# Two score products of a unit, issued together or with transposes or value products between them

## The chip, the cores and the metric

One core of one Trainium2 chip runs the whole program. The metric is the device time of one execution in microseconds (us), as a median over several executions.

## The reference

The reference applies two transformer layers, one after the other, to x of shape (8, 512, 256), with 16 heads of 16 elements. Only the attention of the first layer matters here; the second has the same outline with a key mask in place of the distance term.

```python
qkv = (h @ Wqkv).reshape(B, L, 3, H, hd)             # h: layer norm of x, scaled and shifted
scores = jnp.einsum('bhqd,bhkd->bhqk', q, k) / np.sqrt(hd)
scores = scores - torus_dist[:, None, :, :] * torus_scale[None, :, None, None]
attn = jax.nn.softmax(scores, axis=-1)
out = jnp.einsum('bhqk,bhkd->bhqd', attn, v)
x = x + out @ Wout
x = x + (jax.nn.gelu(layer_norm(x) @ W1 + b1) @ W2 + b2)
```

## The kernel before, in words

The kernel writes every engine's instruction stream by hand and ties the streams with semaphores. It goes through 16 passes: passes 0 to 7 are the first layer, one batch row each, and passes 8 to 15 the second layer. The second layer has a short form, taken when the mask lets all keys but the last 128 drop out of consideration, and with these inputs it is the one that runs. The change touches the code that the first 8 passes use. (The long form of the second layer shares this code, but doesn't run here.)

A pass of the first layer has 37 steps, k = 0 to 36. Its attention is cut into 32 units; a unit is one head and one half of the queries (256 of them). A unit goes through these stages.

- **Scores** (TensorE, `scores`, L869): two products of 97 rows, each 128 queries by 512 keys. They alternate between two PSUM banks, so the product t may start when VectorE has read the product t - 2 (`scores_used`). Unit k is computed in step k. Units 0 and 1 of the next pass are computed ahead, in steps 33 and 35. After the first pass, units 18 and 21 are computed in the middle of the dense work of steps 17 and 20.
- **Shift** (VectorE, `shift_scores`, L1401): for each product, it combines the product with the bias and keeps the row extremum, 128x512 elements, about 0.69 us. The bias is made on GpSimd (`make_bias`, L624), for every fourth unit on ScalarE (L1101), and lies in one of two buffers.
- **Subtract** (GpSimd, `subtract_max`, L631): two operations a unit, into `shifted`.
- **Turn** (TensorE, `turn_unit`, L881): eight 128x128 transposes, four to a PSUM bank. The four of a bank are called a pair here. Unit u is turned in step u + 2. It waits for GpSimd (`shifted_ready`), and each pair z waits until ScalarE has read the pair z - 2 (`probs_ready`).
- **Exponential** (ScalarE, `exps`, L1112): one operation for each pair.
- **Value products** (TensorE, `attend`, L896): for four units at once, 32 instructions, in steps 7, 11, 15, 19, 23, 27, 31 and 35. Two steps later come two transposes (L905), and VectorE divides (L1422, L1426).

TensorE works strictly in the order of its list. In each step that order is: the two scores, then the value products if it is their step, then the eight transposes, then the two transposes of the output, then dense pieces from the table `FIRST` (up projection L777, output projection, query and key projection) and pieces of the down projection from `FIRST_DOWN` (L797). VectorE's step is: divide, the two shifts, the dense pieces of the step before, then a part of a layer norm (`FIRST_NORM`, steps 4, 6, 11 and 13). ScalarE's step k is: the output copy, the dense pieces of step k, the exponentials of unit k - 1, and a bias for unit k + 2 where that is its turn. The table of step 15 holds `t2`, two groups of transposes for the second norm, each of which costs ScalarE two operations ahead of the exponentials. Steps 17 and 20 hold four up projections each, and ScalarE loads another table of functions there and loads the first back afterwards.

SyncE loads the query and key rows of a group of eight units when the scores of an earlier group are ready (`load_group`).

Of the kernel before, what the change touches and what calls it, by code (L numbers as in the profile page):

```python
# [18 lines left out]
def build(nc, d, out):  # L19
    B, L, D = d["x"].shape  # L20
# [15 lines left out]
    UNITS = 2 * H  # L36
    HALF = L // 2
    GQ = 2 * G
# [24 lines left out]
    AHEAD = {33: 0, 35: 1}  # L63
# [25 lines left out]
    ATTEND = 7  # L89
# [3 lines left out]
    TURN = 2  # L93
# [3 lines left out]
    def begun(n, u):  # L97

        return 0 < n < B and u in AHEAD.values()

    def amid(n, k):
        return n > 0 and k in AMID
# [24 lines left out]
    def pieces(table, k, n):  # L127
        return [(p, pass_of(p, n)) for p in table.get(k, []) if pass_of(p, n) is not None]

    with ExitStack() as ctx:  # L130
# [6 lines left out]
        def sem(name):  # L137
            return ctx.enter_context(nc.semaphore(name))
# [124 lines left out]
        s = {name: sem(name) for name in names}  # L263

        def short(n):
            return n >= B and not chosen["any"]
# [506 lines left out]
        def _(pe):  # L773
# [14 lines left out]
            def down_chunks(m, first, last):  # L788
                for i, c in (divmod(x, FCH) for x in range(first, last)):
                    piece = ("down", i)  # L790
                    if i == 0 and c == 0:
                        for last_up in range(DENSE):
                            piece_read(pe, ("up", FCH - 1 - last_up), m)
                        pe.wait_ge(s["down_loaded"], 48 if m < B else 96)
                    if c == 0:
                        bank_free(pe, piece, m)
                    mm = pe.matmul(bank_of(piece, m)[:, 0:D], hidden[:, c, P * i:P * i + P],  # L797
                                   w_down[:, c, :], start=(c == 0), stop=(c == FCH - 1))
                    if c == FCH - 1:
                        mm.then_inc(s["dense_ready"], 1)  # L800
# [56 lines left out]
            def rows_loaded(n, g):  # L857
                pe.wait_ge(s[f"group{g % 2}_loaded"], ROWS_LOADED * (2 * n + g // 2 + 1))

            def scores(n, u):  # L860
                g, half, j = u // 8, u // 4 % 2, u % 4
                if u % 8 == 0:
                    rows_loaded(n, g)
                for i in range(2):
                    t = 2 * u + i
                    if n > 0 or t > 1:
                        pe.wait_ge(s["scores_used"], TILES * n + t - 1)
                    q0 = HALF * half + P * i
                    pe.matmul(score_bank[t % 2], q_rows[0:KROWS, g % 2, j // 2, q0:q0 + P],  # L869
                              k_rows[0:KROWS, g % 2, j // 2, j % 2, :], start=True, stop=True).then_inc(s["scores_ready"], 1)  # L870

            def turn_unit(n, u):
                pe.wait_ge(s["shifted_ready"], UNITS * n + u + 1)
                for pair in range(2):
                    z = 2 * u + pair
                    if n > 0 or z > 1:
                        pe.wait_ge(s["probs_ready"], TILES * n + z - 1)
                    for kk in range(2):
                        kt = 2 * pair + kk
                        for i in range(2):  # L880
                            mm = pe.transpose(turned_bank[z % 2][:, HALF * kk + P * i:HALF * kk + P * i + P],  # L881
                                              shifted[:, u % 3, i, P * kt:P * kt + P], ident[:, :])
                    mm.then_inc(s["turned_ready"], 1)
# [25 lines left out]
            def pair_scores_of(n, q):  # L909

                g, pair = q // 2, q % 2
                if pair == 0:
                    few_loaded(pe, n, g)
                if q > 0 or n > B:
                    pe.wait_ge(s["peaks_ready"], H // 2 * (n - B) + q)
                else:
                    pe.wait_ge(s["scores_used"], TILES * B)
                for t in range(TT):
                    mm = pe.matmul(score[:, t // 2, HALF * (t % 2):HALF * (t % 2) + HALF],  # L919
                                   q_rows[0:KROWS, g, pair, P * t:P * t + P],  # L920
                                   k_rows[0:KROWS, g % 2, pair, :, key_slot(g)], start=True, stop=True)
                mm.then_inc(s["scores_ready"], 2 * TT)

            def turn_peaks(n, q):
                pe.wait_ge(s["split_ready"], H // 2 * (n - B) + q + 1)
                pe.transpose(score_bank[0][0:4 * TT, 0:P], split_peak[:, :].bitcast(F32), ident[:, :])\
                    .then_inc(s["peak_turned"], 1)
# [13 lines left out]
            def attend_heads(n, g):  # L941
                if g == 0:
                    piece_read(pe, ("v", TT - 1), n)
                    pe.wait_ge(s["vmask_ready"], n - B + 1)
                pe.wait_ge(s["probs_ready"], TILES * n + TT * HG * (g + 1))
                pe.wait_ge(s["attn_ready"], GQ * n + 2 * g)
                for j in range(HG):
                    mm = pe.matmul(pv_bank[SLOT * j:SLOT * j + SLOT, :], v_ext[:, TT - 1, HG * g + j, :],  # L948
                                   head_probs[:, (HG * g + j) % RING, :], start=True, stop=True,
                                   skip_group_check=True)  # L950
                mm.then_inc(s["probs_used"], 2)
# [37 lines left out]
            def turn(n):  # L989
                if short(n):  # L990
                    for p in range(HEAD_STEPS):
                        attended = p >= 6 and p % 2 == 0
                        if 2 <= p < 2 + H // 2:
                            pair_scores_of(n, p - 2)
                        for k in range(3 * p, 3 * p + 2):
                            for piece, m in pieces(HEADS, k, n):
                                dense(piece, m)
                            if k in HEADS_DOWN:
                                down_chunks(n - 1, *HEADS_DOWN[k])
                        if attended:  # L1000
                            attend_heads(n, (p - 6) // 2)
                        if 4 <= p < 4 + H // 2:
                            turned_scores_of(n, p - 4)
                        if 2 < p < 2 + H // 2:
                            turn_peaks(n, p - 2)
                        for piece, m in pieces(HEADS, 3 * p + 2, n):
                            dense(piece, m)
                        if p == 2:

                            turn_peaks(n, 0)  # L1010
                        if 3 * p + 2 in HEADS_DOWN:
                            down_chunks(n - 1, *HEADS_DOWN[3 * p + 2])
                        if attended:
                            heads_to_tokens(n, (p - 6) // 2)
                    return
                table, down = (FIRST, FIRST_DOWN) if n < B else (ANY, ANY_DOWN)
                for k in range(STEPS):
                    if k < UNITS and not begun(n, k) and not (n < B and amid(n, k - 1)):
                        scores(n, k)
                    if n + 1 < B and k in AHEAD:  # L1020
                        scores(n + 1, AHEAD[k])
                    if k >= ATTEND and (k - ATTEND) % 4 == 0 and (k - ATTEND) // 4 < GQ:
                        attend(n, (k - ATTEND) // 4)
                    if TURN <= k < TURN + UNITS:
                        turn_unit(n, k - TURN)
                    if k >= TOKENS and (k - TOKENS) % 4 == 0:
                        to_tokens(n, (k - TOKENS) // 4)
                    for i, (piece, m) in enumerate(pieces(table, k, n)):
                        if n < B and amid(n, k) and i == 2:
                            scores(n, k + 1)  # L1030
                        dense(piece, m)
                    if n > 0 and k in down:
                        down_chunks(n - 1, *down[k])
                for gq in range(GQ):
                    if TOKENS + 4 * gq >= STEPS:
                        to_tokens(n, gq)

            def epilogue():
                for piece, m in listed(ANY if chosen["any"] else HEADS, N):
                    dense(piece, m)  # L1040
                down_chunks(N - 1, 0, TT * FCH)

            run(pe, prologue, turn, epilogue)

        @block.scalar
# [576 lines left out]
```

## Time and profile before

| | us |
|---|---|
| median of 3 runs | 1400.09 (1396.74 to 1400.62) |
| the profiled execution's own time | 1405.66 |
| its span, first to last instruction | 1403.9 |
| busy: TensorE matmul | 1294.1 (92%) |
| busy: TensorE weight load | 994.4 (71%) |
| busy: VectorE | 803.9 (57%) |
| busy: ScalarE | 744.4 (53%) |
| busy: GpSimd | 757.0 (54%) |
| mean granted clock of TensorE | 0.982 of 2.4 GHz |

Busy times are unions over the span, and the ends of matmuls are modelled: a busy TensorE isn't one at its peak. What TensorE loses is better read from the starts of its instructions. In a timeline, a row covers a run of instructions of one line (x2 is two); its start is the start of the first, and its duration reaches to the modelled end of the last. The same run takes the same time from start to the next run's start wherever nothing holds it up, so a longer one shows a wait. A single-pass product (scores, up projection) behind a full-precision one (transposes, value products, down projection) is recorded as starting some 0.1 to 0.2 us early, and its successor later by as much; such pairs are compared with their like. The passes begin at 43.7, 127.7, 232.1, 336.6, 441.0, 545.4, 649.8 and 754.2 us.

### The profile page before, as it was taken

Reading aid. Unit: us, or ns where it says so; the run is one execution under the profiler, and the core shown is the slowest. Engines: PE = TensorE matmul, PEld = TensorE weight load, DVE = VectorE, ACT = ScalarE, POOL = GpSimd, SP = SyncE. Lnnn points to the kernel's source line nnn. Section 1 sums busy time; section 2 is a strip of 40 time slices with the busy share of each in tenths; the row PEclk is TensorE's granted clock in tenths of the full one; section 3 lists DMA queues with packets and bytes.
Section 4 is the critical chain, followed back from the end, with each engine's and each line's share of the span. In section 5 each row is a group of like instructions: output and inputs, shape, how many; then the busy total and the mean of one; then the engine's idle time right before and its main releaser. Section 6 shows DMA issues by size and latency. Waiting matters only on the chain.

```text
span 1403.9 us, 24536 instructions
## 1 busy us (share of the span) xinstructions
PE 1294.1 (92%) x8789; PEld 994.4 (71%) x8789; DVE 803.9 (57%) x2240; ACT 744.4 (53%) x1246; POOL 757.0 (54%) x939
## 2 busy tenths in 40 slices
PE   4899999999999999999999998889898989989777
PEld 3577778778778777777778777667666656666656
DVE  3766845746746746746745743565646546564552
ACT  3466765765665665765765663434444444444432
POOL 3698867867877867867867861110403222240323
PEclk9899999999999999999999998999999999999998
DMA  8532332332322322322322324443334242433100
GB/s 259 143 101 74 74 102 54 78 97 54 84 91 54 84 90 54 93 82 54 95 80 76 101 74 122 150 126 135 125 111 165 60 150 77 147 105 118 46 2 30
DMA packets 98259, 133.98 MB, mean 95 GB/s; under 512 B 16802, under 2 KB 51498, under 8 KB 98130
## 3 DMA queue, kind: packets, MB, share of 16 engines
q1 hardware_dynamic: 96850, 131.80, 31.8%
q8 instruction: 73, 1.20, 0.4%
q10 hardware_dynamic: 1280, 0.53, 0.1%
q14 instruction: 56, 0.46, 0.1%
HBM read 72.64 MB, written 58.75 MB: 94 GB/s over the span
## 4 chain that ended last, share of the span: by engine, by line
PE 68%; DVE 19%; issue 4%; DMA 3%; ACT 3%; POOL 2%; SPq 1%; DVEq 0%; POOLq 0%; ACTq 0%
PE dense L777 17%; PE dense L797 15%; PE turned L881 11%; PE pv L896 7%; DVE shifted L1401 6%; PE score L869 6%; DVE x_norm L1241 3%; PE turned L938 2%; PE score L919 2%; PE pv L948 2%; DMA q_rows<-peaks 2%; DVE feat_m L1358 2%; PE dense L785 1%; POOL shifted L631 1%; ACT probs L1112 1%
## 5 line engine op out<-in xcount | busy, mean ns | idle before, releaser
L1401 DVE CUSTOM_DVE_ANT_0 shifted<-score,bias 128x512 f32<-128x512 f32 x512 | 332.1, 686 | 260.3 <-PE score L869 138.7
L631 POOL TENSOR_SCALAR shifted<-shifted,row_max 128x512 f32<-128x512 f32 x512 | 361.1, 718 | 199.8 <-DVE row_max L1401 198.1
L1112 ACT ACTIVATE probs<-turned 128x512 f32<-128x512 f32 x512 | 277.9, 595 | 222.7 <-PE turned L881 222.2
L881 PE MATMUL turned<-ident,shifted 128*128 128x128 f32 x2048 | 270.0, 275 | 6.5 <-POOL shifted L631 6.0
L881 PEld LDWEIGHTS turned<-ident,shifted 128*128 128x128 f32 x2048 | 232.4, 141 | 59.6 <-issue 28.9
L797 PE MATMUL dense<-w_down,hidden 128*128 128x256 f32 x1024 | 258.2, 383 | 0.8 <-ACT hidden L1093 0.8
L624 POOL TENSOR_SCALAR bias<-dist,scale 128x1024 f32<-128x1024 f32 x192 | 218.4, 1138 | 13.8 <-DMA down_bias<-in_L_cond_b 13.8
L869 PE MATMUL score<-k_rows,q_rows 97*128 97x512 f32 x512 | 202.5, 458 | 13.9 <-DMA k_rows<-mask_neg 4.4
L797 PEld LDWEIGHTS dense<-w_down,hidden 128*128 128x128 f32 x1024 | 181.0, 191 | 33.3 <-issue 9.6
L777 PE MATMUL dense<-feat_m,w_up 128*128 128x512 f32 x768 | 188.3, 399 | 1.6 <-DVE feat_m L1358 1.6
L777 PEld LDWEIGHTS dense<-feat_m,w_up 128*128 128x128 f32 x768 | 144.6, 191 | 32.4 <-issue 2.0
L1093 ACT ACTIVATE hidden<-dense,up_bias 128x512 f32<-128x512 f32 x128 | 87.4, 689 | 83.0 <-PE dense L777 82.8
L869 PEld LDWEIGHTS score<-k_rows,q_rows 97*128 97x128 f32 x512 | 92.7, 191 | 48.8 <-DVE row_max L1401 33.9
L896 PE MATMUL pv<-probs,v_ext 128*32 128x256 f32 x2048 | 123.8, 382 | 0.2 <-DVE attn L1426 0.2
L645 POOL CAST mask_colf<-mask_col 128x4 f32<-128x4 uint8 x8 | 1.5, 188 | 211.8 <-PE pv L948 204.1
L777 PE MATMUL dense<-feat_a,w_qkv 128*128 128x512 f32 x384 | 103.5, 410 | 2.8 <-DVE feat_a L1355 2.8
L1128 ACT ACTIVATE probs<-turned 128x512 f32<-128x512 f32 x128 | 69.4, 596 | 56.9 <-PE turned L938 56.8
L896 PEld LDWEIGHTS pv<-probs,v_ext 128*32 128x32 f32 x2048 | 60.2, 109 | 53.9 <-issue 17.2
L1435 DVE TENSOR_REDUCE row_max<-score 128x8 f32<-128x1024 f32 x64 | 78.0, 1220 | 22.5 <-PE score L919 22.5
L777 PEld LDWEIGHTS dense<-feat_a,w_qkv 128*128 128x128 f32 x384 | 70.2, 194 | 16.1 <-issue 3.2
L1080 ACT ACTIVATE qk_high<-dense 128x512 fp32r<-128x512 f32 x64 | 38.3, 599 | 77.1 <-PE dense L777 58.3
L1101 ACT ACTIVATE bias<-dist,scale 128x1024 f32<-128x1024 f32 x64 | 73.7, 1151 | 0.0
(138 smaller groups left out, 1475.6 us busy)
## 6 DMA issues: line engine op xcount, KB each, us to landing
qk_rows<-qk_high SPq DMA_DIRECT2D x128, 256.0 KB
q_rows<-qk_rows SPq DMA_DIRECT2D x64, 384.0 KB
qk_rows<-qk_low SPq DMA_DIRECT2D x64, 256.0 KB
k_rows<-qk_rows SPq DMA_DIRECT2D x68, 192.0 KB
x_in_t<-in_x SPq DMA_DIRECT2D x8, 512.0 KB, 4.8
x_res<-in_x SPq DMA_DIRECT2D x8, 512.0 KB, 5.7
x_mid<-x_norm SPq DMA_DIRECT2D x8, 512.0 KB, 3.3
x_in_t<-x_mid SPq DMA_DIRECT2D x8, 512.0 KB, 4.0
```

The costliest lines, as they stand in the source:

```text
L624: pool.tensor_scalar(bias[:, u % 2, :, :], dist[:, 2 * half:2 * half + 2, :], scale[:, h:h + 1], 0.0, ALU.mult, ALU.add).then_inc(s["bias_ ...
L631: ins = pool.tensor_scalar(shifted[:, u % 3, i, :], shifted[:, u % 3, i, :], -1.0, row_max[:, t % 6:t % 6 + 1], ALU.mult, ALU.add)
L777: mm = pe.matmul(out_ap, left, right, start=(i == 0), stop=(i == len(terms) - 1))
L797: mm = pe.matmul(bank_of(piece, m)[:, 0:D], hidden[:, c, P * i:P * i + P], w_down[:, c, :], start=(c == 0), stop=(c == FCH - 1))
L869: pe.matmul(score_bank[t % 2], q_rows[0:KROWS, g % 2, j // 2, q0:q0 + P], k_rows[0:KROWS, g % 2, j // 2, j % 2, :], start=True, stop=True) ...
L881: mm = pe.transpose(turned_bank[z % 2][:, HALF * kk + P * i:HALF * kk + P * i + P], shifted[:, u % 3, i, P * kt:P * kt + P], ident[:, :])
L896: mm = pe.matmul(pv_bank[SLOT * j:SLOT * j + SLOT, 0:HALF], v_ext[:, kt, HG * (gq // 2) + j, :], probs[:, (4 * gq + j) % RING, kt, :], sta ...
L1093: act.activation(hidden[:, i, :], bank[:, :], ACT.Gelu_apprx_tanh if m < B else ACT.Gelu, bias=up_bias[:, i:i + 1]).then_inc(used(piece, m ...
L1101: act.activation(bias[:, u % 2, :, :], dist[:, 2 * half:2 * half + 2, :], ACT.Copy, scale=scale[:, h:h + 1]).then_inc(s["act_bias_ready"], 1)
L1112: act.activation(probs[:, u % RING, 2 * pair:2 * pair + 2, :], turned_bank[z % 2][:, :].rearrange("p (a c) -> p a c", a=2), ACT.Exp)\
L1401: dve.tensor_tensor_reduce(shifted[:, u % 3, i, :], score_bank[t % 2], bias[:, u % 2, i, :], 1.0, 3.0e38, ALU.add, ALU.min, row_max[:, t % ...
L1435: dve.tensor_reduce(row_max[:, :].rearrange("p (a t) -> p t a", a=2), pair_scores, mybir.AxisListType.X, ALU.max).then_inc(s["peak_ready"], 1)
```

## The change

In a step that computes a unit's scores, only the first score product is issued at the start. Then come the value products, if it is their step, or else the first pair of transposes. Then comes the second score product, and then what is left of the transposes (all eight after value products, the second pair otherwise). The units inside the dense work of steps 17 and 20 keep their two products together, and so do units of other forms of the code. The waits keep their places at the instructions they belong to.

```diff
-            def scores(n, u):
+            def scores(n, u, tiles=range(2)):
                 g, half, j = u // 8, u // 4 % 2, u % 4
-                if u % 8 == 0:
+                if u % 8 == 0 and tiles[0] == 0:
                     rows_loaded(n, g)
-                for i in range(2):
+                for i in tiles:
...
-            def turn_unit(n, u):
-                pe.wait_ge(s["shifted_ready"], UNITS * n + u + 1)
-                for pair in range(2):
+            def turn_unit(n, u, pairs=range(2)):
+                if pairs[0] == 0:
+                    pe.wait_ge(s["shifted_ready"], UNITS * n + u + 1)
+                for pair in pairs:
...
                 for k in range(STEPS):
+                    unit = None
                     if k < UNITS and not begun(n, k) and not (n < B and amid(n, k - 1)):
-                        scores(n, k)
-                    if n + 1 < B and k in AHEAD:
-                        scores(n + 1, AHEAD[k])
-                    if k >= ATTEND and (k - ATTEND) % 4 == 0 and (k - ATTEND) // 4 < GQ:
+                        unit = (n, k)
+                    elif n + 1 < B and k in AHEAD:
+                        unit = (n + 1, AHEAD[k])
+                    attended = k >= ATTEND and (k - ATTEND) % 4 == 0 and (k - ATTEND) // 4 < GQ
+                    turned = TURN <= k < TURN + UNITS
+
+                    if unit:
+                        scores(*unit, range(1))
+                    if attended:
                         attend(n, (k - ATTEND) // 4)
-                    if TURN <= k < TURN + UNITS:
-                        turn_unit(n, k - TURN)
+                    elif turned:
+                        turn_unit(n, k - TURN, range(1))
+                    if unit:
+                        scores(*unit, range(1, 2))
+                    if turned:
+                        turn_unit(n, k - TURN, range(2) if attended else range(1, 2))
                     if k >= TOKENS and (k - TOKENS) % 4 == 0:
                         to_tokens(n, (k - TOKENS) // 4)
```

## Rows read from the trace of the kernel before

**Rows 1.** Busy time by stretch: one at half clock, the first pass, the fourth pass.
```profile
core 0: us, PE busy (x) PEld busy (x) DVE busy (x) ACT busy (x) POOL busy (x), PEclk, DMA share, GB/s
42.70:49.50 6.80, 5.83 (x21) 5.17 (x22) 4.80 (x12) 1.55 (x3) 3.83 (x5) 0.50 0.57 200
43.70:127.70 84.00, 79.61 (x653) 58.82 (x653) 57.09 (x176) 52.53 (x93) 76.52 (x96) 0.97 0.39 116
336.60:441.00 104.40, 102.69 (x803) 81.29 (x801) 63.13 (x194) 65.22 (x110) 77.96 (x97) 1.00 0.28 77
```

**Rows 2.** The score line L869: idle time before it, us and times.
```profile
  DVE row_max L1401: 37.8, 91
```

**Rows 3.** Timeline of TensorE, fourth pass, steps 7, 11, 13 and 15.
```profile
349.98 0.63 PE L869 MATMUL score<-k_rows,q_rows 97*128 97x512 f32 x2
350.54 1.93 PE L896 MATMUL pv<-probs,v_ext 128*32 128x256 f32 x32
...
360.37 1.09 PE L869 MATMUL score<-k_rows,q_rows 97*128 97x512 f32 x2
...
366.98 0.63 PE L869 MATMUL score<-k_rows,q_rows 97*128 97x512 f32 x2
367.44 1.04 PE L881 MATMUL turned<-ident,shifted 128*128 128x128 f32 x8
...
372.81 1.11 PE L869 MATMUL score<-k_rows,q_rows 97*128 97x512 f32 x2
373.85 1.93 PE L896 MATMUL pv<-probs,v_ext 128*32 128x256 f32 x32
375.72 1.09 PE L881 MATMUL turned<-ident,shifted 128*128 128x128 f32 x8
```

**Rows 4.** Timeline of VectorE, fourth pass, shifts of units 11 to 14.
```profile
362.67 0.69 DVE L1401 CUSTOM_DVE_ANT_0 shifted<-score,bias 128x512 f32<-128x512 f32 x1
...
365.48 0.66 DVE L1401 CUSTOM_DVE_ANT_0 shifted<-score,bias 128x512 f32<-128x512 f32 x1
...
367.52 0.69 DVE L1401 CUSTOM_DVE_ANT_0 shifted<-score,bias 128x512 f32<-128x512 f32 x1 [0.77 <-PE score L869]
...
372.06 0.68 DVE L1401 CUSTOM_DVE_ANT_0 shifted<-score,bias 128x512 f32<-128x512 f32 x1
```

**Rows 5.** Timeline of ScalarE, fourth pass, exponentials of units 14, 17 and 19.
```profile
380.06 1.07 ACT L1112 ACTIVATE probs<-turned 128x512 f32<-128x512 f32 x2
...
393.29 1.09 ACT L1112 ACTIVATE probs<-turned 128x512 f32<-128x512 f32 x2 [0.56 <-PE turned L881]
...
403.14 1.08 ACT L1112 ACTIVATE probs<-turned 128x512 f32<-128x512 f32 x2
```

**Rows 6.** Timeline of TensorE, fourth pass, steps 17, 19, 20 and 22.
```profile
378.82 1.12 PE L869 MATMUL score<-k_rows,q_rows 97*128 97x512 f32 x2
380.79 1.06 PE L881 MATMUL turned<-ident,shifted 128*128 128x128 f32 x8 [0.85 <-POOL shifted L631]
...
392.60 1.09 PE L881 MATMUL turned<-ident,shifted 128*128 128x128 f32 x8
...
394.04 1.06 PE L881 MATMUL turned<-ident,shifted 128*128 128x128 f32 x8
...
403.88 1.07 PE L881 MATMUL turned<-ident,shifted 128*128 128x128 f32 x8
```

**Rows 7.** Weight loads of scores and transposes: ns min/median/max, first and last start.
```profile
L869 PEld LDWEIGHTS score<-k_rows,q_rows x512: 186/190/338, 43.6 to 845.9; 97*128 97x128 f32 x171
...
L881 PEld LDWEIGHTS turned<-ident,shifted x2048: 137/141/226, 48.5 to 853.0; 128*128 128x128 f32 x187
```

**Rows 8.** Timeline of TensorE, second layer: value products, then two products of 512 columns.
```profile
906.44 1.07 PE L948 MATMUL pv<-probs,v_ext 128*32 128x512 f32 x8
907.43 0.73 PE L938 MATMUL turned<-q_rows,k_rows 101*128 101x512 f32 x2
```

**Rows 9.** Timeline, GpSimd's subtraction of unit 23 and its transposes in step 25.
```profile
407.50 1.37 POOL L631 TENSOR_SCALAR shifted<-shifted,row_max 128x512 f32<-128x512 f32 x2 [0.37 <-DVE row_max L1401]
...
412.55 1.04 PE L881 MATMUL turned<-ident,shifted 128*128 128x128 f32 x8
```

## The prediction

> **What bounds the kernel now.** I read four views: the page, busy time by stretch, who the score line waits for, and then the timelines of one pass, engine by engine. The page and the stretches say that TensorE hardly rests. In [rows 1] a pass is 104.40 us long, TensorE is busy for 102.69 of it, VectorE for 63.13 and GpSimd for 77.96. The passes from the second to the seventh are alike to 0.1 us, so one pass can be studied and multiplied. The first pass is shorter (84.00 us), for it has no back half of a pass before it to work on, and there GpSimd is busy for 76.52 us. That pass belongs to GpSimd, mostly.
>
> What a reorder on TensorE can win is TensorE's waiting. [Rows 2] count it where the change aims: 37.8 us in 91 waits, 0.42 us each, in which a score product stands until VectorE has read its bank. That is 2.7% of the span. The timeline shows what one such wait is. In step 13 nothing is late: from the start of the two scores to the start of the transposes it is 0.46 us (366.98 to 367.44). In step 7, the way to the value products is 0.56 us (349.98 to 350.54). In step 15 the same way takes 1.04 us (372.81 to 373.85) [rows 3], so 0.48 us are lost at the second product, which waits for VectorE to finish the one before it.
>
> **The change part by part.** No instruction is added or taken away, on any engine or queue. TensorE's list alone is reordered, in some 30 of the 37 steps of each of 8 passes. I follow one full pass, with all numbers as shifts against before (minus is earlier).
>
> *Where it gains.* The second product now comes 0.44 us (four transposes) or 1.9 us (value products) after the first, and VectorE needs 0.62 us a product. So the wait at the second product goes, and its time is used. But VectorE then sets the pace. The chain back is short: a shift that starts on VectorE lets TensorE start the next product in that bank 0.85 us later (I see 0.75 from 372.06 to 372.81 [rows 3, 4], plus 0.1 us because a product that waited is recorded early), and the product reaches VectorE 0.54 us after its start (366.98 to 367.52 [rows 3, 4]). In steps 4 to 8 VectorE has two more operations of the third transpose group and a norm, and runs nearly without rest, so what TensorE wins there is waited for again at the next first product. What is kept is the last of these waits, about 0.3 us of the 0.42 of [rows 2]. The first score of step 11, recorded at 360.37 [rows 3], then comes 0.27 us earlier.
>
> Steps 11 to 15 can be followed product by product. Step 11 has value products. Its first score would truly start at 360.2, its value products at 360.5, the second score at 362.5, and it is on VectorE at 363.04. Before, that shift started at 362.67 [rows 4], so here the split makes VectorE later by 0.37 us. A norm follows, and unit 12's first shift goes from 365.48 to 365.85. The first score of step 13 needs that shift plus 0.85 us, 366.70, instead of 366.98: shift -0.28. In step 13 the second score, behind four transposes, is 0.06 us later on VectorE than back to back, which leaves -0.22 us on the shift of unit 14 (372.06 [rows 4]) and on the first score of step 15. Step 15 loses its own wait at the second product. The part of it that was wait was 0.48 us; 0.37 of it is won after the recording offset of 0.1. The weight load that nothing hides after value products (below) takes 0.10 back, and the transposes of step 15 start 0.50 us before 375.72 [rows 3]. Up to here: **-0.5 us a pass**.
>
> *Where it loses.* The first pair of transposes now stands ahead of the second score. It also waits, for ScalarE to have read the pair two before. Before, both scores were done while it waited. Now only the first is, and the second comes after, 0.24 us on the path. This needs a step whose first pair is bound by ScalarE, and each pass has three that aren't repaid later:
> - Step 17: ScalarE has the two norm groups before it, its exponential starts at 380.06 [rows 5], and the transposes start at 380.79 although the scores started at 378.82 [rows 6]. (The page's releaser is GpSimd, but it had finished that unit long before. It was the other wait.) +0.24.
> - Step 20: it follows value products and has no dense work before it. Transposes start at 392.60, their exponential at 393.29, half of the 1.09 us later the bank is free, and the next transposes start at 394.04 [rows 5, 6]. The loop of 1.44 us is just filled now; with one score less it isn't. +0.24.
> - Step 22: ScalarE comes back from loading its table, exponential at 403.14, transposes at 403.88 [rows 5, 6]. +0.24.
> Step 12 has the same loss as step 20, but the wait for VectorE in step 13 covers it. It is in the sum above.
>
> *Changes of kind.* Scores are single-pass products, transposes full precision. The runs that I compared cost some 0.01 us for each further change of kind. Seven steps are not covered by a stall behind them: +0.08. Value products are followed by a score in place of a transpose. For that the nearest rows are in the second layer: two products behind value products last 0.73 us [rows 8] against 0.63 in step 13 [rows 3], so 0.10 for the weight load that nothing hides. Transposes behind value products last 1.09 against 1.04 [rows 3], 0.05. The difference is 0.05 us, in five uncovered steps (19, 23, 27, 31, 35): +0.25. Bounds: nothing, if the array drains in the shadow; 0.1 each at most, the whole of the first figure, so 0 to +0.5.
>
> The weight load itself differs in the trace: 190 ns for the scores and 141 for the transposes, both of 128 columns [rows 7]. The Trainium skill, TensorE: Matmul & The Clock Gate, section LDWEIGHTS, says that the time depends on the number of columns alone, 107 ns for 128. By it the +0.25 would be nothing, and the whole sum some 2 us lower. The trace doesn't agree with it here, and the trace decides.
>
> *What lies under cover.* In attended steps VectorE gets the second score up to 1.3 us later, and GpSimd its second subtraction. After 407.50 GpSimd needs 1.37 us for unit 23, and TensorE wants it at 412.55 [rows 9]: 3.7 us in hand, less 1.3. So nothing, and if that cover were gone, 1.3 us a step. The group loads of SyncE wait for the second score of units 7 and 15 and are issued up to 1.3 us later. They are needed a group of eight steps on, over 20 us later. In the first pass GpSimd is the bound and continuous, and a later second subtraction starves it by at most 0.15 us in each of some four periods, against small gains at its start: +0.4.
>
> *Sum.* One full pass: -0.50 + 0.72 + 0.08 + 0.25 = +0.55 us. Seven of them: +3.8. With the first pass: **+4.2 us**. The second layer is untouched. Against the profiled execution's own 1405.66 us (1403.9 span, 1.8 around it) this is 1409.9. That execution was 5.6 us above the median of the runs, 1400.09, which becomes 1404.3. Within 0.3% (4.2 us), about what a measurement of this kernel can tell from no change, is exactly the edge.
>
> **The rivals.**
> - *The waits go and stay gone.* VectorE has 41 us of rest in a pass [rows 1], so one may say that it catches up. Then a third of [rows 2] or more is won without the losses, some 9 to 12 us: 1390. Against it: the rest lies in other steps, and in steps 4 to 15 VectorE is late. 0.13.
> - *Gain and loss cancel.* ScalarE's exponentials start earlier too, since the first pair is turned sooner, and steps 17 and 22 recover half: 1400. 0.12.
> - *The late second product turns critical.* In attended steps the second shift, second subtraction, and two steps later the transposes come 1.3 us late. Its place is step 9 to 13 or 25, its price up to 1.3 us in one step of each pass, 8 x 1.3 = 10: 1412 to 1415. It decides once the 2.4 us in hand are gone, as after a norm on GpSimd. 0.12.
> - *The clock falls.* The granted clock is 1.00 (2.4 GHz) in the fourth pass and was 0.50 (1.2 GHz) for 6.8 us at the start [rows 1], behind a TensorE that was half idle. If steps 16 and 17, mostly transposes and a longer wait, brought one such stretch in each pass, it would cost 3.4 us of work each, 24 us: 1424. 0.03. The Trainium skill, the same page, Part 4: PE-mode transpose, says that transposes don't count as busy for the clock. By that rule the fall would be likelier; but in this trace eight in a row, with a wait of over 1 us, haven't brought it.
>
> **How the numbers follow.** My forecast has 0.60, with its own range 1400.5 to 1408: the bounds of 0 to 0.5 on changes of kind and +-0.3 us a pass on the gain. Half of it and more lies above 4.2 us (0.33 slower, 0.27 same). With the rivals: faster 0.14, same 0.39, slower 0.47. The range that holds 8 in 10 leaves out most of the first rival and of the last two: 1396.5 to 1411.
>
> **What would show it.** Right: the starts of two scores in a step lie some 0.7 us apart, and 2.2 around value products; the score line waits for VectorE for about half of 37.8 us; in steps 17, 20 and 22 the transposes start where they did against ScalarE's exponential, and the step is 0.24 us longer; a full pass is 104.9 to 105.0 us. Wrong: a pass under 104.2 us, or first scores in steps 5 to 9 that don't wait; or transposes in step 9, 13 or 25 that wait for GpSimd; or a granted clock of 0.5 inside a pass.

## The result and the profile after

Five runs of the changed kernel have a median of 1407.81 us (1403.54 to 1408.86), five of the kernel before 1399.67 us (1396.74 to 1400.62). The ratio is 1.0044, with a 95% interval of 1.0026 to 1.0063: slower by 6.2 us (the two medians alone lie 8.1 us apart). I had forecast 1404.3 us, 4.2 us slower, in a range of 1396.5 to 1411.

The two profiled executions differ by only 2.1 us (span 1406.0 against 1403.9). The granted clock is 0.982 in both. The passes tell where: the eight passes end 5.2 us later than before, at 862.9 us in place of 857.7, and the second layer, whose code is unchanged, took 543.1 us in this execution and 546.1 in that of before. In the other profiled runs of this study it took between 537 and 546 us. The second layer therefore hides or feigns a change of this size, and I read the change from the passes, which within one execution repeat to 0.1 us. Each kernel was profiled once; steps that an edit leaves alone agree between the kernels to 0.02 us.

From the page after, the busy times:

```profile
PE 1289.8 (92%) x8789; PEld 996.4 (71%) x8789; DVE 814.6 (58%) x2240; ACT 760.2 (54%) x1246; POOL 756.1 (54%) x939
```

Busy time by stretch after, fourth pass; it answers to [rows 1]:

```profile
337.80:443.00 105.20, 102.02 (x804) 81.14 (x801) 64.61 (x194) 67.25 (x110) 77.86 (x98) 1.00 0.28 76
```

The pass is 105.2 us long instead of 104.4. TensorE's matmuls are busy for less of it (102.02 against 102.69) and VectorE for more (64.61 against 63.13), with the same number of instructions. The last is odd, as nothing on VectorE was changed. Half of it (0.75 of the 1.48 us) is in two operations, which come up below: one of the norm of step 13, and `feat_a` in step 10. The rest is that records of neighbouring operations overlap less.

The score line's waits after, which answer to [rows 2]:

```profile
  DVE row_max L1412: 32.5, 67
  issue: 29.9, 61
```

There are 67 waits for VectorE in place of 91, and they still hold 32.5 us of 37.8. I had thought that half would go. But the row adds up idle time of the products and of their weight loads, and most of it is the weight loads': 33.9 of the 37.8 us before, 21.6 of the 32.5 after. So it is not time that TensorE's products lost, and my sign (half of 37.8 us) was not a measure of it. Of the 61 waits of "issue" (7 before), 53 are weight loads of second scores behind value products, 0.41 us each in the fourth pass, with nothing late; the other 8 stand at first scores.

The length of the steps that changed most, from the start of a step's first instruction to that of the next step's, in the timeline of the fourth pass (us):

| step | before | after | | step | before | after |
|---|---|---|---|---|---|---|
| 4 | 2.35 | 2.38 | | 12 | 2.87 | 3.12 |
| 5 | 2.81 | 2.67 | | 14 | 2.89 | 3.29 |
| 6 | 2.52 | 2.16 | | 15 | 4.63 | 4.30 |
| 7 | 3.47 | 3.80 | | 17 | 9.09 | 9.31 |
| 8 | 2.89 | 2.56 | | 19 | 3.27 | 3.32 |
| 10 | 2.12 | 2.43 | | 20 | 7.50 | 7.71 |
| 11 | 3.73 | 3.43 | | 22 | 2.32 | 2.57 |

All others differ by at most 0.04 (steps 36, 0 and 1 taken together). The whole pass, as the mean of the second to the seventh: 105.17 against 104.42, +0.75. The second to seventh pass are 0.70 to 0.78 us longer each, the eighth 0.9, and the first is 0.5 shorter (83.5 us against 84.0, from its first score).

Steps 20 and 22 show the loss that I had forecast. Timeline of TensorE after; the rows answer to [rows 6]:

```profile
394.79 0.48 PE L869 MATMUL score<-k_rows,q_rows 97*128 97x512 f32 x1
395.37 0.63 PE L882 MATMUL turned<-ident,shifted 128*128 128x128 f32 x4
395.76 0.48 PE L869 MATMUL score<-k_rows,q_rows 97*128 97x512 f32 x1
...
404.69 0.58 PE L869 MATMUL score<-k_rows,q_rows 97*128 97x512 f32 x1
405.44 0.63 PE L882 MATMUL turned<-ident,shifted 128*128 128x128 f32 x4 [0.16 <-ACT probs L1123]
405.82 0.49 PE L869 MATMUL score<-k_rows,q_rows 97*128 97x512 f32 x1
```

And ScalarE's exponentials that release them, which answer to [rows 5]:

```profile
394.63 1.09 ACT L1123 ACTIVATE probs<-turned 128x512 f32<-128x512 f32 x2 [0.62 <-PE turned L882]
...
404.69 1.09 ACT L1123 ACTIVATE probs<-turned 128x512 f32<-128x512 f32 x2
```

In step 20 the transposes come 0.58 us after the one score (394.79 to 395.37), as they came 0.60 after both before. From the exponential to the transposes it is 0.74 us in step 20 and 0.75 in step 22, as before (0.75 and 0.74 [rows 5, 6]). ScalarE sets that moment, and the second score now stands behind it.

### The profile page after: what moved, and what is told of

Its sections match the earlier page's. It is cut to its first block, busy times and chain, and to the rows that moved or that the text cites. A ratio compares the mean times of both kernels' runs of the same rounds, so it can differ in the third digit from the quotient of the medians.

```text
span 1406.0 us, 24536 instructions
## 1 busy us (share of the span) xinstructions
PE 1289.8 (92%) x8789; PEld 996.4 (71%) x8789; DVE 814.6 (58%) x2240; ACT 760.2 (54%) x1246; POOL 756.1 (54%) x939
## 4 chain that ended last, share of the span: by engine, by line
PE 66%; DVE 18%; POOL 5%; ACT 4%; issue 4%; DMA 3%; SPq 1%; DVEq 0%; POOLq 0%; ACTq 0%
PE dense L777 18%; PE dense L797 14%; PE turned L882 10%; PE pv L897 7%; PE score L869 7%; DVE shifted L1412 5%; DVE x_norm L1252 3%; POOL shifted L631 3%; PE score L920 2%; PE turned L939 2%; DMA q_rows<-peaks 2%; PE pv L949 2%; DVE feat_m L1369 2%; PE dense L785 1%; POOL bias L624 1%
## 5 line engine op out<-in xcount | busy, mean ns | idle before, releaser
L1412 DVE CUSTOM_DVE_ANT_0 shifted<-score,bias 128x512 f32<-128x512 f32 x512 | 338.3, 687 | 274.8 <-PE score L869 182.6
L1123 ACT ACTIVATE probs<-turned 128x512 f32<-128x512 f32 x512 | 293.8, 597 | 208.9 <-PE turned L882 198.3
L882 PE MATMUL turned<-ident,shifted 128*128 128x128 f32 x2048 | 296.2, 273 | 15.9 <-POOL shifted L631 10.3
L882 PEld LDWEIGHTS turned<-ident,shifted 128*128 128x128 f32 x2048 | 247.1, 140 | 61.8 <-issue 17.5
L869 PE MATMUL score<-k_rows,q_rows 97*128 97x512 f32 x512 | 246.5, 487 | 15.5 <-DVE row_max L1412 10.9
L869 PEld LDWEIGHTS score<-k_rows,q_rows 97*128 97x128 f32 x512 | 96.8, 189 | 56.3 <-issue 29.9
L1104 ACT ACTIVATE hidden<-dense,up_bias 128x512 f32<-128x512 f32 x128 | 87.3, 688 | 83.8 <-PE dense L777 83.5
L1139 ACT ACTIVATE probs<-turned 128x512 f32<-128x512 f32 x128 | 69.4, 596 | 57.3 <-PE turned L939 57.2
```

Of the source, the lines that this page charges most:

```text
L1104: act.activation(hidden[:, i, :], bank[:, :], ACT.Gelu_apprx_tanh if m < B else ACT.Gelu, bias=up_bias[:, i:i + 1]).then_inc(used(piece, m ...
L1123: act.activation(probs[:, u % RING, 2 * pair:2 * pair + 2, :], turned_bank[z % 2][:, :].rearrange("p (a c) -> p a c", a=2), ACT.Exp)\
L1412: dve.tensor_tensor_reduce(shifted[:, u % 3, i, :], score_bank[t % 2], bias[:, u % 2, i, :], 1.0, 3.0e38, ALU.add, ALU.min, row_max[:, t % ...
```

## The experiments

All start from the changed kernel or the one before. Pass lengths are means of the second to the seventh pass, from the timeline of each (104.42 us before, 105.17 with the change); step lengths are those of the fourth.

**Which places lose: the value products or the first transposes.** Each of these kernels splits only the steps that a condition names, and keeps both scores first in all others. The first splits the steps with value products:

```diff
+                    if not (attended):
+                        if unit:
+                            scores(*unit)
+                        if attended:
+                            attend(n, (k - ATTEND) // 4)
+                        if turned:
+                            turn_unit(n, k - TURN)
+                    else:
+                        if unit:
+                            scores(*unit, range(1))
...
```

The others name the steps without value products; all but 12, 17, 20 and 22; and 17, 20 and 22 alone. A fifth, further down, names 4, 5, 6, 8, 9, 10 and 15.

Only the steps with value products:

> Only the eight steps with value products keep the split; in the others both scores come first, as before. A full pass was 104.43 us before and 105.17 with the change. If the losses are those of the first transposes ahead of the second score (steps 17, 20, 22), they are gone here. Steps 11 and 15 keep their gain of 0.3 to 0.4 us each, the eight weight loads cost 0.05 each, and the late shift of unit 11 costs steps 13 to 15 some 0.3: a full pass of 104.2 to 104.5 us, a ratio to before of 1.000. If instead the value products are the harmful place (the rival), the pass is 104.9 us or more.

Measured: 104.53 us a pass, just above the range, ratio 1.0009 (0.9995 to 1.0022).

Only the others:

> Only the steps without value products keep the split. My theory: steps 17, 20 and 22 are longer by 0.22 to 0.25 us each as in the changed kernel, step 12 too; steps 4 to 10 gain 0.3 to 0.45 in all; step 15 waits again at its second product (its 0.48 us). A full pass of 104.9 to 105.1 us, ratio 1.003 to 1.004. The rival, that the value products do the harm: 104.2 us or less.

Measured: 105.15 us, just above the range, ratio 1.0025 (1.0010 to 1.0041), a little below mine. Step 17 is 9.33 us, step 20 is 7.71, step 22 is 2.57. The rival falls in both: the loss sits with the first transposes. But the two halves don't add up. Alone they cost 0.11 and 0.73 us, together 0.75.

Four steps kept whole:

> The changed kernel with the scores of steps 12, 17, 20 and 22 kept together. My theory: each of the last three gives its 0.22 to 0.25 us back, and step 12's is covered by VectorE as it was or moves the first score of step 13 by nothing: a full pass of 105.17 - 0.7 = 104.4 to 104.5 us, ratio 1.000. The rival, that the time of these steps is set by the order elsewhere (ScalarE late anyway): 105.0 us or more.

Measured: 104.45 us, ratio 1.0007 (0.9991 to 1.0023). Steps 17, 20 and 22 are 9.08, 7.47 and 2.32 us, as before the change. Step 12 whole gave nothing: it is 0.18 us shorter than with the change, but steps 13 and 14 are 0.17 longer. The timeline in step 20:

```profile
393.55 0.71 PE L869 MATMUL score<-k_rows,q_rows 97*128 97x512 f32 x2
394.13 1.07 PE L882 MATMUL turned<-ident,shifted 128*128 128x128 f32 x8
```

The other way round, these three alone split in the kernel before:

> Steps 17, 20 and 22 alone are split, all others as before. Theory: these three are 0.21 to 0.25 us longer each, nothing after them repays it: a full pass of 104.43 + 0.70 = 105.1 us. Rival, that the loss needs the late VectorE of the other split steps: 104.5 us.

Measured: 105.15 us, ratio 1.0046 (1.0030 to 1.0063). Three displaced products alone lose 0.73 us a pass, as much as the full change does in sum (0.75), in which gains and losses elsewhere nearly cancel. Step 17 of this kernel, where the wait is longest:

```profile
380.61 0.50 PE L869 MATMUL score<-k_rows,q_rows 97*128 97x512 f32 x1
382.58 0.63 PE L882 MATMUL turned<-ident,shifted 128*128 128x128 f32 x4 [1.47 <-POOL shifted L631]
382.96 0.48 PE L869 MATMUL score<-k_rows,q_rows 97*128 97x512 f32 x1
```

TensorE rests from the first score to 382.58, and a product that could have run in that rest comes at 382.96. (The releaser named is GpSimd, as in [rows 6]. But GpSimd had ended unit 15 at 378.46 here, and at 376.67 in the kernel before. The exponential begins 0.72 us before the transposes, 0.73 in the kernel before, the same distance as in steps 20 and 22: it is ScalarE.)

**Where a split gains.** Seven steps in which the second score waited for VectorE and no transposes wait for ScalarE:

> Only steps 4, 5, 6, 8, 9, 10 and 15 are split, the places where the second score waited for VectorE before and no first transposes wait for ScalarE behind it. My theory: 0.3 to 0.45 us won by step 10 are partly waited away at step 11, 0.1 to 0.3 of them survive, and step 15 keeps 0.3: a full pass of 103.9 to 104.1 us, ratio 0.995 to 0.998, faster than both. The rival, that VectorE binds again behind every gain: 104.4 us.

Measured: 104.03 us a pass, ratio 0.9990 (0.9974 to 1.0006). In the passes this is 0.39 us each, as expected; in the runs it is no clear difference, and the ratio misses my range. Steps 7 and 10 are as long as in the full change (3.82 and 2.41), and step 4 is 0.14 longer than before, so nearly all that steps 5, 6 and 8 won is gone by step 11. But step 15 keeps its 0.33, and steps 13 and 14 are 2.94 and 2.88 as before.

**Why step 14 grew.** Step 14 is 2.89 us before, 3.29 after, 2.88 with seven steps split, and 2.75 where only steps without value products are. The first score of step 15, which ends it, waits for VectorE's first shift of unit 14, and that shift stands behind the norm of step 13. After the change:

```profile
373.46 0.68 DVE L1412 CUSTOM_DVE_ANT_0 shifted<-score,bias 128x512 f32<-128x512 f32 x1
374.21 0.50 PE L869 MATMUL score<-k_rows,q_rows 97*128 97x512 f32 x1 [0.38 <-DVE row_max L1412]
```

The norm's operations in the fourth pass, VectorE against GpSimd, before:

```profile
368.66 1.12 POOL L624 TENSOR_SCALAR bias<-dist,scale 128x1024 f32<-128x1024 f32 x1
369.35 2.30 DVE L1241 TENSOR_SCALAR x_norm<-x_res,mean_var,rstd 128x256 f32<-128x256 f32 x4
```

and after:

```profile
370.06 1.12 POOL L624 TENSOR_SCALAR bias<-dist,scale 128x1024 f32<-128x1024 f32 x1
370.34 2.70 DVE L1252 TENSOR_SCALAR x_norm<-x_res,mean_var,rstd 128x256 f32<-128x256 f32 x4
```

Four operations of 256 columns take 2.30 us in one and 2.70 in the other. Before, they start 0.69 us into GpSimd's bias of 1.12 us, after, 0.28 us into it. The first of the four takes 0.58 us before and 0.98 after: it ends at 369.93 and 371.32, in both cases shortly after the bias does (369.78 and 371.18). The other three are alike. One of them alone takes 0.40 us where GpSimd rests. Over the kernel's 32 such operations the median is 0.57 us before and 0.78 after.

**Why step 10 grew.** The same stands in step 10, 2.12 us before and 2.43 after. VectorE's `feat_a` comes ahead of the shifts of unit 10, and the first score of step 11 starts when the first of these has ended (360.29 and 360.37 before, 361.35 and 361.42 after). Before:

```profile
357.19 1.12 POOL L624 TENSOR_SCALAR bias<-dist,scale 128x1024 f32<-128x1024 f32 x1
358.11 0.74 DVE L1355 TENSOR_TENSOR feat_a<-hidden,feat_a 128x512 fp32r<-128x512 f32 x1
```

After:

```profile
358.27 1.11 POOL L624 TENSOR_SCALAR bias<-dist,scale 128x1024 f32<-128x1024 f32 x1
358.83 1.08 DVE L1366 TENSOR_TENSOR feat_a<-hidden,feat_a 128x512 fp32r<-128x512 f32 x1
```

Within the pass VectorE came to it 0.47 us earlier than before. It met the bias sooner, took 0.34 us longer, and only 0.13 of the 0.47 was left. In all eleven profiled kernels this operation ends 0.53 or 0.54 us after the bias that it meets. No run moves this bias by itself, so here the cause rests on that match and on the test of the norm that follows.

So the theory: such an operation of VectorE, if it meets GpSimd inside an instruction, can't finish before that instruction has ended. (In the fourth pass, before and after the change, each norm operation that did so ended 0.14 or 0.15 us after it, less than its 0.40 alone: part of it goes on meanwhile.) To test it I halved two of GpSimd's biases, in the changed kernel, in the seven-step kernel and in the one before:

```diff
             def make_bias(n, u):
...
+                if u in (8, 14):
+                    for i in range(2):
+                        ins = pool.tensor_scalar(bias[:, u % 2, i, :], dist[:, 2 * half + i, :], scale[:, h:h + 1],
+                                                 0.0, ALU.mult, ALU.add)
+                    ins.then_inc(s["bias_ready"], 1)
+                    return
                 pool.tensor_scalar(bias[:, u % 2, :, :], dist[:, 2 * half:2 * half + 2, :], scale[:, h:h + 1], 0.0,
                                    ALU.mult, ALU.add).then_inc(s["bias_ready"], 1)
```

> The changed kernel with GpSimd's biases of units 8 and 14 made by two operations of 128x512 in place of one of 128x1024 (same work, one more start each). Theory: an operation of VectorE's norm that meets GpSimd in the middle of an operation waits for that operation's end; it takes 0.40 us alone, 0.78 between subtractions of 0.7 us, and up to 1.20 against a bias of 1.12 us. With halves the first norm operation of step 13 falls from 0.97 to 0.6 us or less and the last one of step 6 from 1.20 to 0.8. Step 14 or 15 and step 7 get up to 0.3 us shorter each: a full pass of 104.6 to 105.0 us instead of 105.17. Rival: the norm is slow for another reason (a wait for data, memory traffic as such), and the operations keep 0.97 and 1.20 us and the pass 105.17.

Measured: 104.79 us a pass instead of 105.17, ratio 1.0038 (1.0025 to 1.0051). The norm of step 6, changed kernel and then halved:

```profile
350.77 2.99 DVE L1252 TENSOR_SCALAR x_norm<-x_in_t,mean_var,rstd 128x256 f32<-128x256 f32 x4
352.48 1.13 POOL L624 TENSOR_SCALAR bias<-dist,scale 128x1024 f32<-128x1024 f32 x1
```
```profile
350.75 2.60 DVE L1258 TENSOR_SCALAR x_norm<-x_in_t,mean_var,rstd 128x256 f32<-128x256 f32 x4
352.50 1.41 POOL L626 TENSOR_SCALAR bias<-dist,scale 128x512 f32<-128x512 f32 x2
```

The last operation fell from 1.20 us to 0.78, and step 7 from 3.80 to 3.40. In step 13 the first fell from 0.98 to 0.55. But there the last one, which had met a resting GpSimd, rose from 0.40 to 0.79, for a subtraction of GpSimd had now started just before it. Step 14, which hangs on it, hardly changed (3.29 to 3.24). The rival is out. The operations follow the length and the phase of GpSimd's instructions.

> The kernel before with the halved biases. Theory: the same operations of the norm get shorter (1.20 to 0.8 in step 6, the first of step 13 keeps about 0.6 as it met the bias near its end), and the first score of step 8 comes 0.2 to 0.4 us earlier: a full pass of 104.0 to 104.3 us instead of 104.43. Rival: unchanged, 104.43.

Measured: 104.16 us a pass. Step 7 is 3.27 us and step 8 is 2.62 (before 3.47 and 2.89), but step 14 rose to 3.12, as the first norm operation of step 13 went from 0.58 to 0.80: it now started 0.03 us into the second half and had that whole half ahead of it. I had expected it to keep its luck. The runs show no difference, 1.0011 (0.9997 to 1.0024), -0.4 to +3.4 us. In the trace the eight passes end 1.5 us earlier than before, which lies outside that; the disagreement isn't explained.

> The kernel with seven split steps (104.03 us a pass), with the halved biases of units 8 and 14. Theory: the last norm operation of step 6 falls from 1.20 to 0.8 us, and the first score of step 8 and with it the pass come 0.2 to 0.4 us earlier; the norm of step 13 gives up to 0.2 more: 103.5 to 103.8 us a pass, ratio to before 0.994 to 0.997. Rival, that the extra start on GpSimd or other waits eat it: 104.0.

Measured: 103.95 us, ratio 0.9988 (0.9975 to 1.0001). That misses the range. Step 7 got its 0.40 us (3.42), step 8 gave 0.15 back, and step 14 0.29 (3.17), by the same operation of the norm, 0.56 to 0.85 us.

**A version that beats both.** The seven-step kernel again, with the bias of unit 8 alone in halves:

```diff
-                if u in (8, 14):
+                if u == 8:
```

> The seven split steps, with the bias of unit 8 alone in halves. In the run with both halved, the first norm operation of step 13 went from 0.56 to 0.85 us; with the one bias of unit 14 it should keep its luck if it still meets the bias near its end. Theory: step 7 is 0.4 us shorter, 0.1 to 0.3 of it survives steps 8 and 10: a full pass of 103.7 to 103.9 us against 103.95 (both halves) and 104.03 (none), ratio to before 0.995 to 0.997. Rival, that the pass is pinned from step 10 on by the norm of step 13: 103.95 to 104.05 us.

Measured: 103.58 us a pass, 0.84 less than before and 1.59 less than with the change, a little under my range. Ratio to before 0.9971 (0.9955 to 0.9987): 4 us faster, clear of the runs' spread. Step 14 is 2.85 us: the first norm operation of step 13 took 0.53 us, still meeting the whole bias near its end. The last one of step 6 took 0.78.

## Why the prediction was right, and where a term was off

**The losses at the first transposes** (+0.24 in each of steps 17, 20 and 22) measured 0.22, 0.21 and 0.25: together 0.68 of my 0.72. The run with these three alone gives +0.73. The mechanism is shown from both sides, by taking them out and by having nothing else. Step 12 was to be covered by VectorE, and was: it is 0.25 longer, the first score of step 13 came 0.20 us earlier than before (forecast 0.28), and with step 12 whole, steps 12 to 14 take 9.36 us in place of 9.37.

**The changes of kind** (+0.08 and +0.25) measured as follows. Steps 19, 23, 27 and 31, with value products, are 0.03 to 0.05 longer each and step 35 is 0.01 longer; steps 24, 25, 26, 28 and 29 are 0.01 to 0.02 longer, and steps 30 and 33 are not. Together that is 0.25, or 0.2 with the 0.04 that steps 36, 0 and 1 are shorter, instead of 0.33. The 0.05 for a score behind value products came out near 0.04, and 0.01 in step 35; that the weight loads of 190 against 141 ns are its cause, no run shows. By the rule of the Trainium skill (TensorE: Matmul & The Clock Gate, section LDWEIGHTS) that columns alone decide a weight load's time, the two kinds of load would last equally long; the trace says otherwise [rows 7].

**The gain** (-0.50) was the term that was mis-sized: steps 2 to 16 gave -0.12 us. Counted from the first score of step 2, the first score of step 11 came 0.14 us earlier (forecast 0.27), the transposes of step 11 0.39, unit 12's first shift 0.39 later (forecast 0.37), and the first score of step 13 0.20 earlier (forecast 0.28). The failing step is the sentence that unit 14's shift and the first score of step 15 would come 0.22 us earlier: the score came 0.21 us later. I had carried the durations of VectorE's operations over unchanged. The norm of step 13 started 0.20 us earlier and took 0.40 longer, by its meeting with GpSimd, and +0.20 is what the score shows. Step 10 had lost in the same way: `feat_a` took 0.34 us longer there, and kept the gain at step 11 to 0.14. In the run with value products alone the late VectorE shows by itself. Step 13 is 0.50 longer (3.44 us), as its second score stood until unit 12's second shift had ended (367.73, the score at 367.79), and the first norm operation took 1.06 us and step 14 2.99.

**The first pass** was put at +0.4 and came out 0.5 us shorter, the eighth 0.9 longer; I followed neither step by step. From first score to end the first pass took between 83.5 and 84.5 us in the kernels of this study, each profiled once, so the cause of 0.5 us stays open.

**Sum.** Forecast 0.55 a pass, measured 0.75. Of the difference, +0.38 is the gain that was too large, and the other terms give back 0.18. That the total came near is partly luck: these errors cancel in part, and the first pass was wrong the other way. 5.2 us over the eight passes agrees with the 6.2 us (3.6 to 8.8) that the runs show.

**The rivals.** That the waits go and stay gone is refuted: first scores still wait for VectorE, 0.38 us at step 15 alone, and even with no loss at the transposes (four steps kept whole) the pass is 104.45 us, not below 104.42. (A third of 37.8 us is 12.6, not the 9 to 12 that I wrote.) That steps 17 and 22 recover half by earlier exponentials didn't happen: they lost 0.22 and 0.25 in full. That the late second product becomes critical at the transposes two steps later didn't happen; after step 22 no attended step grew by more than 0.05. It did have a cost, by another way: the late second shifts moved VectorE against GpSimd. The clock was granted at 1.00 throughout the fourth pass.

## What to carry to other kernels

Splitting a pair of products to fill a wait pays only where the instruction moved ahead isn't itself waiting. Where it waits, the product that used to run in that wait is added to the path in full; here three of some 30 places cost more than all others gained (+0.68 against -0.12 a pass in steps 2 to 16). So decide place by place: find for each step which wait ends last, split there, and leave the rest whole. Where VectorE runs ops that stall against GpSimd, a shift by a few tenths of a microsecond upstream can be lost again or return larger, and a long GpSimd instruction near such ops is worth cutting in two, if the phase behind it is checked.

## What the runs showed of the hardware

VectorE's norm operation (fp32, one input in SBUF, one output in SBUF, 128x256) takes 0.40 us where GpSimd rests. It takes 0.78 us, one at a time between GpSimd's instructions, where GpSimd is subtracting (0.70 us each), and 1.20 us against a bias of 1.13 us. Its end follows the end of the GpSimd instruction that it met, not the bytes moved: with the bias cut in half, the 1.20 us became 0.78, with the same bytes moved. The shifts, which read their scores from PSUM, stay between 0.65 and 0.70 us in all 512 cases. The Trainium skill, SBUF — State Buffer, section Who interferes with whom, says that VectorE in a two-port mode, which such an operation can enter, and GpSimd hold a shared pair of ports for a whole instruction, and the other blocks. The trace agrees with the blocking: in the fourth pass, before and after the change, each norm operation that met GpSimd ended 0.14 or 0.15 us after the instruction it met. That these operations ran in such a mode, no trace here shows. It could have been read from the profile before, where the same line's four operations took 0.50, 0.78, 0.78 and 1.20 us in step 6.

Operations of VectorE with two inputs in SBUF met GpSimd too, and there the trace shows it both ways. `feat_a` took 0.74 to 1.08 us in step 10, always ending 0.53 or 0.54 us after GpSimd's bias. And three subtractions of GpSimd in the fourth pass, in both kernels, took 1.12 or 1.13 us instead of 0.70; each had started while VectorE was in such an operation (two with 0.80 us, one with 0.74 before and 1.08 after) and ended 0.56 or 0.57 us after it.
